# Two attention layers on one core: the output biases as GpSimd rows summed by a matmul of ones

## The reference, cut to what matters

```
xn   = group_norm(x, 32 groups) * gamma + beta      # eps 1e-5 in the first layer, 1e-6 in the second
q    = xn @ wq + bq ;  k = xn @ wk + bk ;  v = xn @ wv + bv
attn = softmax(q @ k.T / sqrt(256))                 # 1024 x 1024 for each image
x    = (attn @ v) @ wp + bp + x                     # the second layer calls them wo and bo
```

## Time and profile before

| what | value |
|---|---|
| runs | 250.44, 252.51, 252.88 us; median 252.51 us |
| profiled execution | 250.97 us, its span 249.2 us, granted TensorE clock 0.999 |
| PE busy | 244.8 us (98% of the span) |
| PE weight loads busy | 222.8 us (89%) |
| DVE busy | 189.3 us (76%) |
| ACT busy | 149.2 us (60%) |
| POOL busy | 125.2 us (50%) |

### The profile page before, as it was taken

The page is one execution under the profiler, slowest core; times in us unless marked ns, Lnnn a source line. Parts: engine busy times, 40 slices in busy tenths (PEclk is TensorE's granted clock), DMA queues, the critical chain, the costliest instruction groups (busy, mean ns, idle before and its releaser), DMA issues.

```text
span 249.2 us, 4565 instructions
## 1 busy us (share of the span) xinstructions
PE 244.8 (98%) x1558; PEld 222.8 (89%) x1558; DVE 189.3 (76%) x500; ACT 149.2 (60%) x291; POOL 125.2 (50%) x151
## 2 busy tenths in 40 slices
PE   8999999999999999999999999999999999999995
PEld 7898889889998899889998899889998899889994
DVE  0588899999994798588976998589885798449804
ACT  2665444799994309841998409940998519740920
POOL 3010530685779306901797916901797918700870
PEclk9999999999999999999999999999999999999999
DMA  6999000000025002320132001320110000100102
GB/s 196 333 171 231 0 0 3 0 1 3 0 93 80 1 0 55 81 34 3 43 84 43 3 0 45 86 42 4 42 43 0 3 21 24 42 0 17 49 22 84
DMA packets 34766, 12.36 MB, mean 50 GB/s; under 512 B 26284, under 2 KB 34488, under 8 KB 34744
## 3 DMA queue, kind: packets, MB, share of 16 engines
q1 hardware_dynamic: 34720, 12.07, 19.5%
q10 hardware_dynamic: 24, 0.01, 0.0%
HBM read 7.88 MB, written 4.19 MB: 48 GB/s over the span
## 4 chain that ended last, share of the span: by engine, by line
PE 98%; ACT 0%; DVE 0%; issue 0%; DVEq 0%
PE ring L1168 12%; PE ring L1170 12%; PE ring L1169 12%; PE ring L1144 12%; PE ring L1142 12%; PE ring L1143 12%; PE ring L1128 3%; PE ring L1130 3%; PE ring L1129 3%; PE ring L1116 3%; PE ring L1117 3%; PE ring L1115 3%; PE ring L991 2%; PE ring L982 1%; PE ring L1066 1%; PE ring L1000 1%
## 5 line engine op out<-in xcount | busy, mean ns | idle before, releaser
L369 POOL TENSOR_TENSOR P_lo<-S,P_hi 128x512 fp32r<-128x512 f32 x64 | 81.9, 1307 | 49.6 <-ACT S L509 49.3
L1168 PE MATMUL ring<-V,P_hi 128*128 128x258 f32 x256 | 72.3, 282 | 0.0
L1170 PE MATMUL ring<-V,P_lo 128*128 128x258 f32 x256 | 72.2, 282 | 0.0
L1169 PE MATMUL ring<-V,P_hi 128*128 128x256 f32 x256 | 72.2, 282 | 0.0
L508 ACT ACTIVATE P_hi<-S 128x512 fp32r<-128x512 f32 x64 | 40.2, 628 | 29.7 <-DVE S L831 29.7
L501 ACT COPY S<-ring 128x512 f32<-128x512 f32 x64 | 36.5, 590 | 31.3 <-PE ring L1144 30.3
L1142 PE MATMUL ring<-t_hi,xn_lo 128*128 128x512 f32 x128 | 49.9, 390 | 0.0
L1144 PE MATMUL ring<-t_hi,xn_hi 128*128 128x512 f32 x128 | 49.9, 390 | 0.0
L1143 PE MATMUL ring<-t_lo,xn_hi 128*128 128x512 f32 x128 | 49.8, 389 | 0.0
L1168 PEld LDWEIGHTS ring<-V,P_hi 128*128 128x128 f32 x256 | 48.4, 189 | 0.4
L1169 PEld LDWEIGHTS ring<-V,P_hi 128*128 128x128 f32 x256 | 48.3, 189 | 0.5
(11 more groups left out here) (128 smaller groups left out, 357.0 us busy)
## 6 DMA issues: line engine op xcount, KB each, us to landing
xnat<-in_x SPq DMA_DIRECT2D x8, 256.0 KB, 4.0
between<-xnat SPq DMA_DIRECT2D x16, 128.0 KB, 1.8
out<-xnat SPq DMA_DIRECT2D x16, 128.0 KB, 1.7
moved<-in_x SPq DMA_DIRECT2D x8, 128.0 KB, 4.4
moved<-between SPq DMA_DIRECT2D x16, 64.0 KB, 2.4
moved<-between SPq DMA_DIRECT2D x32, 32.0 KB, 2.0
w_wq<-in_L_conv_wq SPq DMA_DIRECT2D x2, 256.0 KB, 4.6
w_wk<-in_L_conv_wk SPq DMA_DIRECT2D x2, 256.0 KB, 4.8
```

The costliest lines, as they stand in the source:

```text
L369: nc.gpsimd.tensor_tensor(P_lo[:, exp_of(c, kb), :], S[:, tile_of(c, kb), :], P_hi[:, exp_of(c, kb), :].bitcast(F32), ALU.subtract).then_i ...
L1168: nc.tensor.matmul(bank[:, 0:C + 2], P_hi[:, tile, mine], v[:, kb, 0:C + 2], start=(kb == 0), stop=False)
L1169: nc.tensor.matmul(bank[:, 0:C], P_hi[:, tile, mine], v[:, kb, C + 2:VX], start=False, stop=False)
L1170: last = nc.tensor.matmul(bank[:, 0:C + 2], P_lo[:, tile, mine], v[:, kb, 0:C + 2], start=False, stop=(kb == NB - 1))
```

## The change

The biases in the middle of the output are formed in another way:

- POOL multiplies the rows of wp by the entries of bv, one per partition (two instructions on 128x256), adds the two channel blocks, and splits the sum into a high and a low fp32r part: five instructions for each layer, ten in all (`weighted_rows`). They stand in POOL's list behind `power(0)` and a new wait for dv_xl to reach 4, and ahead of the wait for dv_ob.
- PE no longer runs `output_bias` (both layers). `output_biases_to_all` is now two matmuls of 512 columns with a 128x128 tile of ones as the stationary operand, which sum the 128 rows and lay the sum out on all partitions. They write bank X instead of ring[6], wait for the tenth count of po_bv and for the fourth of dv_Wx, and stand in front of score block 5 of chunk 0 instead of in front of block 0.
- DVE no longer runs `bias_columns`. `output_biases` is two additions of 128x256 (X plus bp, one for each layer) instead of one copy, behind the running maximum of score block 5 instead of ahead of `Wx_low(1)`. bp comes as a third row of `wide`, so each of the two `wide` transfers is half as large again. DVE also fills the tile of ones at the start.
- The score block that takes ring[6] no longer waits for dv_ob. The transposes of R wait for dv_ob instead of dv_Wx. `maxima_by_query(0)` comes behind the values of block 4 instead of 2, `shift_to_all(0)` behind those of 7 instead of 6, and `query_maxima(0)` behind `v_low` of block 3 instead of 2.

```diff
-WIDE = VECTORS[3:5]
+WIDE = VECTORS[3:6]
...
# POOL
+            def weighted_rows(l):
+                r = l * NV + VECTORS.index("bv")
+                pool.wait_ge(ld_w[l, "wp"], 16)
+                for k in range(KC):
+                    nc.gpsimd.tensor_scalar(weighted[:, l, k, :], w_raw[l, "wp"][:, k, :], vec_cols[:, k, r:r + 1],
+                                            None, ALU.mult).then_inc(po_bv, 1)
+                pool.wait_ge(po_bv, 5 * l + 2)
+                nc.gpsimd.tensor_tensor(weighted[:, l, 0, :], weighted[:, l, 0, :], weighted[:, l, 1, :], ALU.add
+                                        ).then_inc(po_bv, 1)
+                pool.wait_ge(po_bv, 5 * l + 3)
+                nc.gpsimd.tensor_copy(weighted_hi[:, l, :], weighted[:, l, 0, :]).then_inc(po_bv, 1)
+                pool.wait_ge(po_bv, 5 * l + 4)
+                nc.gpsimd.tensor_tensor(weighted_lo[:, l, :], weighted[:, l, 0, :], weighted_hi[:, l, :].bitcast(F32),
+                                        ALU.subtract).then_inc(po_bv, 1)
...
             power(0)
+            pool.wait_ge(dv_xl, TQ)
+            weighted_rows(0)
+            weighted_rows(1)
             pool.wait_ge(dv_ob, 1)
...
# DVE
+            nc.vector.memset(ones[:].bitcast(F32), 1.0)
...
-            def bias_columns():
-                dve.wait_ge(pe_ob, LAYERS)
-                for l in range(LAYERS):
-                    nc.vector.tensor_tensor(bias_col[:, l, :], bias_bank(l), vec_cols[:, :, l * NV + VECTORS.index("bp")],
-                                            ALU.add).then_inc(dv_oc, 1)
...
             def output_biases():
                 dve.wait_ge(pe_oa, 1)
-                nc.vector.tensor_copy(out_bias[:, :, :], ring[RING - 1][:, :].rearrange("p (l c) -> p l c", l=LAYERS)
-                                      ).then_inc(dv_ob, 1)
+                for l in range(LAYERS):
+                    dve.wait_ge(ld_wide[l], 16)
+                    last = nc.vector.tensor_tensor(out_bias[:, l, :], X[:, l * C:(l + 1) * C],
+                                                   wide[:, l, WIDE.index("bp"), :], ALU.add)
+                last.then_inc(dv_ob, 1)
...
             normalise(0, range(2, 4))
-            bias_columns()
             Wx_low(0, 1)
...
-            output_biases()
             for k in range(KC):
                 Wx_low(1, k)
             statistics_of(1, 0)
...
                 if kb == NR:
                     channel_statistics(1)
+                if kb == NR + 1:
+                    output_biases()
             for m in range(QB):
                 v_low(0, m)
-                if m == 2:
-                    query_maxima(0)
+            query_maxima(0)
             query_shift(0)
...
# PE
-            def output_bias(l):
-                pe.wait_ge(ld_w[l, "wp"], 16)
-                if l:
-                    pe.wait_ge(dv_stat, VARE)
-                r = l * NV + VECTORS.index("bv")
-                for k in range(KC):
-                    for kd in range(KC):
-                        last = nc.tensor.matmul(bias_bank(l)[:, k:k + 1], w_raw[l, "wp"][:, kd, k * P:(k + 1) * P],
-                                                vec_cols[:, kd, r:r + 1], start=(kd == 0), stop=(kd == KC - 1))
-                last.then_inc(pe_ob, 1)
...
             def output_biases_to_all():
-                pe.wait_ge(dv_oc, LAYERS)
-                for l in range(LAYERS):
-                    for k in range(KC):
-                        last = nc.tensor.transpose(ring[RING - 1][:, l * C + k * P:l * C + (k + 1) * P],
-                                                   bias_col[:, l, k:k + 1].to_broadcast([P, P]), ident[:])
-                last.then_inc(pe_oa, 1)
+                pe.wait_ge(po_bv, 5 * LAYERS)
+                pe.wait_ge(dv_Wx, LAYERS * KC)
+                nc.tensor.matmul(X[:], ones[:], weighted_hi[:, :, :].rearrange("p l c -> p (l c)"),
+                                 start=True, stop=False)
+                nc.tensor.matmul(X[:], ones[:], weighted_lo[:, :, :].rearrange("p l c -> p (l c)"),
+                                 start=False, stop=True).then_inc(pe_oa, 1)
...
                     if ring_place[tile] == RING - 1:
-                        pe.wait_ge(dv_ob, 1)
+                        pe.wait_ge(dv_stat, VARE)
...
             transpose_weight(0, 2)
-            output_bias(0)
             mean_of_groups()
...
             transpose_weight(1, 2)
-            output_bias(1)
             for mc in range(KC):
                 A_product(1, mc)
...
-                    pe.wait_ge(dv_Wx, LAYERS * KC)
+                    pe.wait_ge(dv_ob, 1)
...
-            output_biases_to_all()
             for kb in range(NB):
+                if kb == 5:
+                    output_biases_to_all()
                 scores(0, kb)
             for m in range(NB):
                 values(0, m)
-                if m == 2:
+                if m == 4:
                     maxima_by_query(0)
-                if m == 6:
+                if m == 7:
                     shift_to_all(0)
```

More of the change, by code:

```diff
@@ L121, in two_attention_layers @@
         eps = sb("eps", [P, LAYERS])
-        bias_col = sb("bias_col", [P, LAYERS, KC])
+        ones = sb("ones", [P, P], F32R)
         out_bias = sb("out_bias", [P, LAYERS, C])
@@ L170, in two_attention_layers @@
             products = sb("products", [P, LAYERS, NATT, C], stack=early)
+            weighted = sb("weighted", [P, LAYERS, KC, C], stack=early)
+            weighted_hi = sb("weighted_hi", [P, LAYERS, C], F32R, stack=early)
+            weighted_lo = sb("weighted_lo", [P, LAYERS, C], F32R, stack=early)
         P_hi = sb("P_hi", [P, P_TILES, BANK], F32R)
@@ L189, in two_attention_layers @@
         po_bk = sem("po_bk")
+        po_bv = sem("po_bv")
         po_resid = sem("po_resid")
@@ L199, in two_attention_layers @@
         pe_Wx = sem("pe_Wx")
-        pe_ob = sem("pe_ob")
         pe_oa = sem("pe_oa")
@@ L227, in two_attention_layers @@
         dv_Wx = sem("dv_Wx")
-        dv_oc = sem("dv_oc")
         dv_ob = sem("dv_ob")
@@ L245, in two_attention_layers @@
         dv_O = sem("dv_O")
-        def bias_bank(l):
-            return ring[RING - 1][:, (l + 1) * KC:(l + 2) * KC]
         def mean_bank(v):
```

## The result

The changed kernel takes 252.45 us (median of 22 runs, 251.39 to 254.67) against 251.0 us for the kernel before (22 runs). The ratio is 1.0055, interval 1.0041 to 1.007: slower by some 1.4 us, where 0.85 us less was forecast. On the median of before measured here, the forecast would have been 250.15. The median that stood ahead of the prediction, 252.51 us from three runs, was itself 1.5 us too high.

What follows compares the result with a forecast made beforehand. PE (98% busy, no recorded wait after 10 us) was taken to bound the kernel. Its terms -0.05 - 0.81 - 0.45 + 0.46 gave -0.85 us, from a median of 252.51 to 251.66 us, range 249.6 to 253.0.

Steps and rivals of the forecast that it cites:

- The wait ahead of the group means: PE, layer 0's output_bias removed: about 0.78 us becomes waiting for DVE's channel statistics, only 0.05 is gained.
- the gain up to t_product: PE, both output_bias blocks removed: 0.05 plus 0.81 us, so t_product starts at 18.04 instead of 18.90.
- the margins of the low parts of x: DVE's first two low parts are ready 0.4 and 0.6 us before PE needs them, so the 0.86 is kept.
- transposes and matmuls of ones cancelling: PE: removing the bias transposes saves 0.45 us, the two added matmuls with ones cost 0.46.
- the weighted rows in time: POOL's ten added instructions take 8.3 us and end near 29.9, before PE needs them at 31.5.
- the transfers at the start: Both wide loads grow from 256 to 384 KB, up to 1.5 us for both; nothing here reaches PE.
- the residual's end: POOL's residual, moved later, starts near 36.7 and ends at 42.4 us, with cover of about 1.8.
- Shift to all: PE reaches shift_to_all at 42.2 us, DVE has the query shift ready at 41.2: margin 1.0.
- rival 1: DVE's two query-shift operations each wait out a POOL instruction, PE waits 0.5 us: -0.35, 252.2 us; chance 0.12.
- The reordering: DVE's last maximum ends near 38.2 us, PE's later transposes of R come at 39.6: no wait.
- Rival 2: PE's removed products give nothing, as A_product of layer 1 has an unseen reason: 0 change, 252.5 us; chance 0.10.
- Rival 3: PE waits before score block 5 for late weighted rows, from 0.90 us an instruction: +3.2, 255.8 us; chance 0.08.

Runs made afterwards that it cites:

- e1: Changed kernel with the old order of the chunk 0 maximum (transposes of R, shift_to_all, query_maxima) put back: 251.10 us, ratio 1.0008 to the kernel before.
- e5: Kernel before plus one DVE memset of one column (0.06 us) at about 1 us: 251.23 us, ratio 1.0014 to the kernel before.
- e9: Changed kernel whose rearranged loads for units 2 and 3 read x and do not wait for the stores: 251.45 us, ratio 1.0027 to the kernel before.
- e8: Kernel before without PE's products of bv and wp in both layers, DVE's instruction count kept: 250.72 us, ratio 0.9974 to the kernel before.
- e2: Changed kernel with ones matmuls before score block 4 and DVE's additions behind block 3's maximum, so the residual ends earlier: 251.21 us, ratio 1.0032 to the kernel before.
- e3: Changed kernel with both the old order of the chunk 0 maximum and the earlier bias matmuls and additions: 250.91 us, ratio 0.9992 to the kernel before.
- e7: Changed kernel with old maximum order, earlier bias matmuls and additions, and one DVE wait instruction removed: 250.27 us, ratio 0.9980 to the kernel before.
- e11: The same kernel as e7, measured again to narrow its interval: 250.32 us, ratio 0.9987 to the kernel before.

## Why the prediction was wrong

**Right, and by its own numbers.** The wait ahead of the group means (0.67, "about 0.7"); the gain up to t_product (0.90 without the loads, for 0.86); the margins of the low parts of x; transposes and matmuls of ones cancelling; the weighted rows in time (8.2 for 8.3, though made up differently: 0.92 for a multiplication by a column, 0.40 for a cast, against 0.74 for both, and one addition of 1.01); the transfers at the start; the residual's end. At 43 us PE had 0.68 of its 0.85, or 0.79 without the later loads.

**The step that failed** is "Shift to all", and with it rival 1. Both asked whether neg_shift would be ready for PE's `shift_to_all`. It was, though by 0.19 us and not 1.0 (42.28 against 42.47). Neither asked what stands behind neg_shift on DVE's own list. Rival 1 had the mechanism but not the size (two waits for a POOL instruction, 1.5 us; the two operations took 0.68 more than before), and it put the damage at the wrong consumer: nothing at 42 us, everything at 69, where the values of unit 1 take the banks that DVE's divisions free. There the lead of 0.59 went and 0.98 more. The reordering, which I costed at nothing since its margins against PE were positive, is worth 0.71 us by e1 in the trace, and by the ratios (1.0055 to 1.0008) 1.2.

**What was luck.** The measured 252.45 lies inside the range of 249.6 to 253.0, and near the 252.2 of rival 1, only because the range and the rivals stood on 252.51 for the kernel before. Against the kernel before, rival 1 said 0.35 us less, and 1.4 us more came.

**Why I did not see it.** That whatever leaves PE's list shortens the time, if nothing that PE waits for is late, was checked up to 65 us only. An absence of waits is not slack. The steps of 0.18 and 0.23 in the values of unit 1 of the kernel before told that slack was nil; four rows of DVE beside them would have priced it.

**Not foreseeable from the trace of before:** the stop at two divisions, which one DVE instruction more brings (0.36 by e5), how often a store lands late (0.7 by the ratios of e9 and the changed kernel), and the slower step of the values blocks (0.20 in unit 0).

**Rival 2** (removal gives nothing) is refuted by the changed kernel's own start of t_product and by e8. **Rival 3** needed 0.90 us an instruction on the mean, waits not counted; the ten were busy for 7.72 us, 0.77 each (0.82 with the waits between them, 8.16 / 10), and PE found them ready. A time above that of the kernel before was forecast by rival 3 alone, and it came for another reason.

## What to carry to other kernels

When the bounding engine shows no waits, price the slack of each engine that hands it buffers before moving work around: find where its steps are a few hundredths longer than usual, and follow the second engine's list from every place that the change touches to its next consumer, not only to the nearest. If small DVE operations with two SBUF inputs are due, keep GpSimd's long element-wise instructions away from them. And when a time moves by a few tenths for an edit that should cost nothing, count instructions: try one more or one less. When two traces are compared stage by stage, take off first what the loads at the start differ by; here that was up to 0.5 us between versions whose edits were worth 0.7.

## What the hardware showed

- DVE operations of four columns with both inputs in SBUF took 0.34 and 0.66 us instead of 0.16 beside GpSimd additions of 0.74, and ended with them; with the additions moved away (e2, e3) they took 0.16. The Trainium skill (SBUF — State Buffer, SBUF: two separate sides) has such operations wait for a GpSimd instruction in progress to its end, and these rows agree.
- DVE stopped 0.46 to 0.48 us ahead of a division that waits for its own reciprocal, in each of the seven profiles where the division was the 192nd or 320th recorded DVE instruction, and in none of the six where it was the 191st or 319th. At the 448th and 512th no such stop shows.
- GpSimd took 0.92 us for a 128x256 multiplication by one value per partition, 0.74 for an addition of two tensors (1.01 for one that started at 23.57, together with a DVE product of two SBUF inputs) and 0.40 for a cast to fp32r.
- The same store of 128 KB landed 1.7 us after its issue in one execution and 4.0 us in another of the same kernel (e7, e11).
- A values block of unit 0 took 0.738 us in the changed kernel, (39.81 - 36.12) / 5, against 0.713 before. It is not the residual beside it: in e2 and e3 the matmuls still step 0.122 us behind the residual's end, against 0.119 in the kernel before. The cause is open.
